# An attention block and a soft mixture of experts in one program: the attention's and the front's steps merged into one list an engine

## The reference, cut to what matters

```python
# attention (B=8, T=512, C=256, 16 heads, latent 32)
q_lat, k_lat, v_lat = (t @ w.T + b for each head)      # rope on q_lat and k_lat
q_for_k = q_lat @ wqk_w.T + wqk_b
att = softmax(mask(einsum('bhql,bhkl->bhqk', q_for_k, k_lat) * L ** -0.5))
y   = heads(einsum('bhqk,bhkl->bhql', att, v_lat) @ l2o_w.T + l2o_b)
x1  = layernorm(x + y @ cproj_w.T + cproj_b)
# soft mixture of experts
z      = layernorm(x1) ; xn = z * norm_g + norm_b
logits = einsum('bnd,esd->bnes', xn, layernorm(slot_embeds) * slot_g + slot_b)
dispatch = softmax(logits, over tokens) ; combine = softmax(logits, over all slots)
slots  = einsum('bnd,bnes->besd', xn, dispatch)
eout   = (gelu(slots @ Wg + bg) * (slots @ Wu + bu)) @ Wd + bd
out    = layernorm(x1 + einsum('bns,bso->bno', combine, eout))
```

## Time and profile before

| | before |
|---|---|
| time, median of 3 (us) | 1336.6 (1336.46 to 1337.25) |
| the profiled execution: time, span (us) | 1336.36, 1334.5 |
| TensorE matmul busy | 1215.3 us, 91% |
| VectorE, ScalarE, GpSimd busy | 61%, 51%, 34% |
| TensorE's mean granted clock | 0.96 |

### The profile page before, as it was taken

One profiled execution on the slowest core, in us unless ns is written; L12 is line 12 of the kernel. 1 busy time (PEld: TensorE's weight loads), 2 busy tenths in 40 slices (PEclk: granted clock), 3 DMA queues, 4 the chain that ended last, 5 costly groups with the idle time before them and its releaser, 6 DMA issues.

```text
span 1334.5 us, 19895 instructions
## 1 busy us (share of the span) xinstructions
PE 1215.3 (91%) x7190; PEld 944.3 (71%) x7222; DVE 814.2 (61%) x1318; ACT 682.2 (51%) x1042; POOL 449.5 (34%) x336
## 2 busy tenths in 40 slices
PE   5798999999999999973799999994999999999996
PEld 4465666666656666632688888883888888888885
DVE  3877697979787978631577777763444444432343
ACT  2545464646465656451667777762555555540111
POOL 5544555555545555410100000000444444430000
PEclk9898999999999999976899999997999999999998
DMA  3644353636363645411123333234554545453661
GB/s 121 139 104 111 90 158 87 163 90 159 89 157 91 158 97 134 107 49 63 48 95 111 111 112 112 96 104 152 195 165 166 164 166 165 165 193 95 225 247 47
DMA packets 121790, 170.30 MB, mean 128 GB/s; under 512 B 47025, under 2 KB 76146, under 8 KB 121714
## 3 DMA queue, kind: packets, MB, share of 16 engines
q1 hardware_dynamic: 120818, 168.74, 43.4%
q10 hardware_dynamic: 896, 0.56, 0.1%
HBM read 72.26 MB, written 37.75 MB: 82 GB/s over the span
## 4 chain that ended last, share of the span: by engine, by line
PE 51%; DVE 3%; ACT 2%; DMA 1%; issue 1%; POOL 1%; SPq 0%; ACTq 0%; POOLq 0%; DVEq 0%
PE ring L361 8%; PE ring L363 8%; PE ring L362 7%; PE ring L1438 6%; PE tail L361 3%; PE tail L363 3%; PE tail L362 3%; PE tail L1438 2%; PE ring L1365 2%; PE ring L1348 1%; PE ring L1355 1%; PE tail L1285 1%; PE ring L1274 1%; PE ring L1307 1%; PE tail L1355 1%
## 5 line engine op out<-in xcount | busy, mean ns | idle before, releaser
L738 ACT ACTIVATE pt<-ring 128x1024 f32<-128x1024 f32 (+1 forms) x192 | 169.2, 882 | 148.7 <-PE ring L1274 137.1
L983 DVE TENSOR_REDUCE mx<-ring 128x4 f32<-128x512 f32 (+2 forms) x192 | 197.7, 1039 | 77.6 <-PE ring L1259 77.3
L628 POOL TENSOR_SCALAR_AFFINE_SELECT pt<-pt 128x512 f32<-128x512 f32 x128 | 81.2, 634 | 248.2 <-ACT pt L738 248.2
L1274 PE MATMUL ring<-qks 98*128 98x256 f32 (+3 forms) x512 | 131.6, 361 | 10.3 <-DVE mx L983 4.8
L1257 PE MATMUL ring<-qks 96*128 96x384 f32 (+3 forms) x512 | 139.9, 362 | 0.9 <-DVE mx L983 0.6
L1274 PEld LDWEIGHTS ring<-qks 98*128 98x128 f32 x512 | 77.6, 195 | 69.1 <-DVE mx L983 28.8
L1285 PE MATMUL tail<-pt,va 128*32 128x512 f32 (+3 forms) x1024 | 99.8, 463 | 11.6 <-POOL pt L628 9.8
L653 POOL TENSOR_TENSOR hl<-hid,hh 128x512 fp32r<-128x512 f32 x64 | 82.6, 1302 | 78.4 <-ACT hh L824 78.4
L639 POOL TENSOR_TENSOR zl<-z,zh 128x1024 fp32r<-128x1024 f32 x8 | 19.3, 2410 | 242.9 <-ACT zh L777 242.9
L1257 PEld LDWEIGHTS ring<-qks 96*128 96x128 f32 x512 | 92.2, 199 | 10.9 <-ACT pt L738 6.1
L1097 DVE SCALAR_TENSOR_TENSOR hid<-ring,bias_e,gate 128x512 f32<-128x512 f32 x64 | 47.9, 748 | 83.3 <-ACT gate L818 51.9
(11 more groups left out here) (217 smaller groups left out, 3114.0 us busy)
## 6 DMA issues: line engine op xcount, KB each, us to landing
qks<-stg SPq DMA_DIRECT2D x384, 128.0 KB, 2.4
c_dram<-c2s SPq DMA_DIRECT2D x32, 512.0 KB, 5.2
c<-c_dram SPq DMA_DIRECT2D x32, 512.0 KB, 5.9
sl_dram<-sls SPq DMA_DIRECT2D x32, 256.0 KB, 3.4
sl<-sl_dram SPq DMA_DIRECT2D x16, 512.0 KB, 4.8
wg<-in_wg SPq DMA_DIRECT2D x16, 512.0 KB, 5.6
wu<-in_wu SPq DMA_DIRECT2D x16, 512.0 KB, 6.2
wd<-in_wd SPq DMA_DIRECT2D x16, 512.0 KB, 7.0
```

What stands on the lines that cost most here:

```text
L628: nc.gpsimd.affine_select(out=m, in_=m, compare_op=ALU.is_ge, fill=0.0, base=0, pattern=[[0, GH], [1, P]], channel_multiplier=-1).then_inc ...
L738: nc.scalar.activation(pt[j % 2][:, h:h + heads, 0:n], heads_of(tile, heads, n), ACT.Exp, scale=SCALE).then_inc(empty, 1)
L983: nc.vector.tensor_reduce(out=mx[:, g, i, h:h + heads], in_=heads_of(tile, heads, (i + 1) * P), axis=AX.X, op=ALU.max).then_inc(empty, 1)
L1274: last = nc.tensor.matmul(scores[:, h, :], qks[0:KS_ROWS + 2, g, h0 + h, 1, j * P:(j + 1) * P], qks[0:KS_ROWS + 2, g, h0 + h, 0, j * P:T], ...
```

## The change

`attn_order` becomes `order(at, window, start)`: it puts the steps of the front's windows at positions of their own, 16.3 a round, into the same sorted list. Each engine has a start for them (PE and SP 264, ACT 263, DVE 261), where attention of batch 7 has the positions from 224 on. The second loops over the front's steps go away on PE, ACT, DVE and SP; GpSimd keeps its own. Front steps thus stand among the steps of batch 7's groups: s1 of batch 0 among the exp of group 2, round 0 among those of group 3 and the projection, cproj, ln and apply of batch 7 in round 1.

`fills` numbers all fills together: the three ring places in turn, and the tail pair from the last misc or pv step on; the first fill of the tail waits until misc and ybank are drained. z is loaded once its own batch's store has landed, and the first two also once xt and v of batch 7 were read. SP's window has z behind the slots stores. New waits name the last readers of what lies under each front buffer, and the attention's and the front's buffers get new addresses, which set what those last readers are. The names quad_slot and quad_count become slot and fill_count throughout (not shown).

```diff
+FRONT_AT, FRONT_ACT_AT, FRONT_DVE_AT, FRONT_SPAN = 264, 263, 261, 16.3
...
-def attn_order(at):
+def order(at, window=(), start=FRONT_AT):
...
+    for w in range(-2, B + 1):
+        for n, (name, ahead, *more) in enumerate(window):
+            if 0 <= w + ahead < B:
+                todo.append((start + FRONT_SPAN * (w + n / len(window)), len(todo), (name, w + ahead, *more)))
     return [step for _, _, step in sorted(todo)]
 
 
-def front_order(window):
-
-    steps = []
-    for w in range(-1, B + 1):
-        for name, ahead, *n in window:
-            if 0 <= w + ahead < B:
-                steps.append((name, w + ahead, *n))
-    return steps
+def fills(steps):
+
+    free, left = list(range(RING)), [0] * QUAD
+    slot_of, turn_of = {}, {}
+    last = max(n for n, s in enumerate(steps) if s[0] in MISC_STEPS + ("pv",))
+    for n, s in enumerate(steps):
+        if n == last:
+            free.insert(0, RING)
+        if s[0] in PAIR_STEPS:
+            r = free.pop(0)
+            free.append(r)
+            slot_of[s], turn_of[s] = r, left[r]
+            left[r] += 1
+    return slot_of, turn_of, left
...
-SP_FRONT = (("z", 2), ("c2", 0, 0), ("c2", 0, 1), ("slots", -1, 1), ("slots", 0, 0), ("c2", 0, 2), ("c2", 0, 3))
-
-PAIR_STEPS = ("lat", "max", "exp", "v", "yTT", "cproj", "wv", "seT")
+SP_FRONT = (("c2", 0, 0), ("c2", 0, 1), ("slots", -1, 1), ("z", 2), ("slots", 0, 0), ("c2", 0, 2), ("c2", 0, 3))
+
+PAIR_STEPS = ("lat", "max", "exp", "v", "yTT", "cproj", "wv", "seT", "zT", "s1", "s2", "d", "c2", "slots")
...
+    pe_steps = order(PE_AT, PE_FRONT)
+    slot_of, turn_of, FILLS = fills(pe_steps)
+    misc_no = {s: n for n, s in enumerate(s for s in pe_steps if s[0] in MISC_STEPS)}
...
+    lat = place("lat", [P, 2, T], f32)
+    rot = place("rot", [P, 2, T], f32)
+    rope = place("rope", [P, 2, T], f32)
     cos = place("cos", [P, T], f32)
     sin = place("sin", [P, T], f32)
-    blat = place("blat", [P, 2, G], f32)
+    stg = [place(f"stg{i}", [P, 4, T], f32r) for i in range(2)]
+    qks = place("qks", [P, G, GH, 2, T], f32r)
+    mts = [place(f"mts{i}", [2 * GH, T], f32r) for i in range(2)]
+    identb = place("identb", [P, P], bf16)
+    maskb = place("maskb", [P, GH, P], bf16)
+    wq = place("wq", [P, P], f32)
     bwq = place("bwq", [P, 1], f32)
     bv = place("bv", [P, C], f32)
+    va = place("va", [P, NT, H, L], f32)
+    temp_at = at[0]
+    pt = [place(f"pt{i}", [P, GH, T], f32) for i in range(2)]
+    ys = place("ys", [P, T], f32)
+    ytok = place("ytok", [P, NT, C], f32)
+    yT_ = place("yT_", [P, NC, T], f32)
+    x = [place(f"x{i}", [P, NT, C], f32) for i in range(2)]
+    x1 = place("x1", [P, NT, C], f32)
...
+    s1s, c1, dh, dl = [], [], [], []
+
+    def rows_of(i):
+        s1s.append(place(f"s1s{i}", [P, NT, E * S], f32))
+        c1.append(place(f"c1{i}", [P, NT, E * S], f32))
+
+    def dispatch_of(i):
+        dh.append(place(f"dh{i}", [P, NT, 512], f32r))
+        dl.append(place(f"dl{i}", [P, NT, 512], f32r))
+
+    assert at[0] <= xt_at + 36 * KB
+    rows_of(0)
+    c2s = [place(f"c2s{i}", [P, 2, T], f32) for i in range(2)]
     e2 = [place(f"e2{i}", [P, 2, T], f32) for i in range(4)]
-    dh = [place(f"dh{i}", [P, NT, 512], f32r) for i in range(2)]
-    dl = [place(f"dl{i}", [P, NT, 512], f32r) for i in range(2)]
-    c2s = [place(f"c2s{i}", [P, 2, T], f32) for i in range(4)]
+    dispatch_of(0)
+    rows_of(1)
+    dispatch_of(1)
+    c2s += [place(f"c2s{i + 2}", [P, 2, T], f32) for i in range(2)]
     sls = [place(f"sls{i}", [P, NC, 512], f32) for i in range(2)]
-    m1 = place("m1", [P, 2, NT], f32)
-    cs = place("cs", [P, 2, NT], f32)
-    m2 = place("m2", [P, NT, 2], f32)
-    es = place("es", [P, NT, 2], f32)
-    res = place("res", [P, NT, 2], f32)
-    assert at[0] <= nc.sbuf_usable_end - 16 * KB
+    assert at[0] <= temp_at + 26 * KB
...
+    def last_read(engine, g):
+        read = ("exp", B - 1, g, len(EXP_UNITS) - 1)
+        engine.wait_ge(pair_filled[slot(read)], fill_count(read))
...
+            def load_z(b):
+                sp.wait_ge(z_stored, (b + 1) * 16)
+                sp.dma_start(z[b % 2][:, :, :], z_dram[b, :, :]).then_inc(z_loaded[b % 2], 16)
+
+            for st in order(SP_AT, SP_FRONT):
                 name, b = st[:2]
...
-            sp.wait_ge(z_stored, B * 16)
-            sp.wait_ge(x1_stored, B * 16)
-            load_z(0)
...
+                elif name == "z":
+                    if b < 2:
+                        for read in (("lat", B - 1, G - 1), ("v", B - 1)):
+                            sp.wait_ge(pair_filled[slot(read)], fill_count(read))
                         load_z(b)
                     else:
-                        sp.wait_ge(quad_filled[quad_slot(("zT", b - 2))], quad_count(("zT", b - 2)))
+                        sp.wait_ge(pair_filled[slot(("zT", b - 2))], fill_count(("zT", b - 2)))
                         sp.wait_ge(z_low, b - 1)
                         load_z(b)
...
-            for st in attn_order(ACT_AT):
+            for st in order(ACT_AT, ACT_FRONT, FRONT_ACT_AT):
...
+                    if (b, n) == (0, 0):
+                        act.wait_ge(cosed, B * G)
+                        act.wait_ge(roped, B * G)
+                        act.wait_ge(k_low, B * G)
+                        act.wait_ge(misc_filled, misc_count(("wqk", B - 1, G - 1)))
+                        for g in range(G):
+                            act.wait_ge(stacked[g], B * 3 * GH * 16)
+                    elif (b, n) == (1, 0):
+                        last_read(act, G - 1)
+                        act.wait_ge(y_filled, B * G)
                     nc.scalar.activation(s1s[b % 2][:, n, :].rearrange("p (k s) -> p k s", k=2), tile[:, :, :], ACT.Copy)
...
+                    if b == 0:
+                        last_read(act, n // 2)
...
+                    elif n < 2:
+                        last_read(act, 1)
+                    else:
+                        act.wait_ge(y_filled, B * G)
...
+                    if b == 0 and n < 2:
+                        last_read(act, 0)
+                    elif b == 0:
+                        act.wait_ge(y_filled, B * G)
+                        act.wait_ge(misc_filled, misc_count(("yT", B - 1, G - 1)))
...
-            for st in attn_order(DVE_AT):
+            for st in order(DVE_AT, DVE_FRONT, FRONT_DVE_AT):
...
+                    if b == 0 and n < 2:
+                        last_read(dve, 2)
+                    elif b == 0:
+                        dve.wait_ge(y_filled, B * G)
...
-            for st in attn_steps:
+            for st in pe_steps:
...
+                    if (slot(st), fill_count(st)) == (RING, 1):
+                        pe.wait_ge(misc_drained, len(misc_no))
+                        pe.wait_ge(y_drained, B * G)
...
-            for r in range(RING):
-                pe.wait_ge(pair_drained[r], FILLS[r])
-            pe.wait_ge(misc_drained, len(misc_no))
-            pe.wait_ge(y_drained, B * G)
-
-            for st in front_steps:
-                name, b = st[:2]
-                tile = quad[quad_slot(st)]
-                full = quad_filled[quad_slot(st)]
-                pe.wait_ge(quad_drained[quad_slot(st)], quad_count(st, 0))
-
-                if name == "zT":
+                elif name == "zT":
```

More of the change, by code:

```diff
@@ L173, in block_kernel @@
     snv, sny, snt, snm = (place(n, [P, 8], f32) for n in ("snv", "sny", "snt", "snm"))
-    temp_at = at[0]
-    pt = [place(f"pt{i}", [P, GH, T], f32) for i in range(2)]
-    ys = place("ys", [P, T], f32)
-    ytok = place("ytok", [P, NT, C], f32)
-    yT_ = place("yT_", [P, NC, T], f32)
-    x = [place(f"x{i}", [P, NT, C], f32) for i in range(2)]
-    x1 = place("x1", [P, NT, C], f32)
+    m1 = place("m1", [P, 2, NT], f32)
+    cs = place("cs", [P, 2, NT], f32)
+    m2 = place("m2", [P, NT, 2], f32)
+    es = place("es", [P, NT, 2], f32)
+    res = place("res", [P, NT, 2], f32)
     at[0] = temp_at
@@ L261, in block_kernel @@
     misc, ybank = tail[:, 0, :], tail[:, 1, :]
-    quad = ring + [tail]
+    pairs = ring + [tail]
     acc = ((ring[0], ring[1]), (ring[2], tail))
@@ L271, in block_kernel @@
     setup_dve = sem("setup_dve")
-    pair_filled = [sem(f"pair_filled{r}") for r in range(RING)]
-    pair_drained = [sem(f"pair_drained{r}") for r in range(RING)]
+    pair_filled = [sem(f"pair_filled{r}") for r in range(QUAD)]
+    pair_drained = [sem(f"pair_drained{r}") for r in range(QUAD)]
     misc_filled, misc_drained = sem("misc_filled"), sem("misc_drained")
@@ L288, in block_kernel @@
     z_loaded = [sem(f"z_loaded{i}") for i in range(2)]
-    quad_filled = [sem(f"quad_filled{r}") for r in range(QUAD)]
-    quad_drained = [sem(f"quad_drained{r}") for r in range(QUAD)]
     z_high, z_low, xn_high, xn_low = sem("z_high"), sem("z_low"), sem("xn_high"), sem("xn_low")
@@ L602, in _ @@
             pool.wait_ge(in_rope, IN_ROPE * 16)
-            for st in attn_order(POOL_AT):
+            for st in order(POOL_AT):
```

(9 more changed lines are left out.)

95 lines of the change are left out of this document (26 added, 69 removed).

## The result

The changed kernel takes 1329.59 us (median of 4 runs, 1328.13 to 1330.48) against 1336.92 us for the kernel before beside it (4 runs, 1336.46 to 1338.24): a ratio of 0.994, interval 0.9925 to 0.996. It is faster by 7.3 us, where 28.6 us were forecast and 1296 us was the low end of the range, 1322 the high end. The direction was right and the size was not. The profiled execution took 1329.52 us (span 1327.8), 6.8 us less than the one of before.

What follows compares the result with a forecast made beforehand. TensorE sets the pace except in a hole where latencies do. Work 99.95 us plus waits 26.9 us makes the 155.4 us stretch 126.8, a gain of 28.6, so 1308 us; range 1296 to 1322.

Steps and rivals of the forecast that it cites:

- I take full clock, since both gaps lie in dense work: TensorE's clock stays at 2.4 GHz through the merged stretch despite gaps at 565.8 and 579 us; nothing charged.
- The rival with the fallen clock: TensorE's clock falls in the merge, between 583 and 606 us: 9 us more, 1317 us; chance 0.18.
- zT(0) crossed on VectorE: VectorE has zT(0) ahead of max (7,2,5) and cproj(6), which TensorE fills in reverse order: 4.0 us of waits.
- layernorm of batch 6: On VectorE it comes some 4 us later, behind xn(0) as well, and holds exp (7,2,1): 3.0 us.
- s1 among the exp: Groups 2 and 3 with batch 0's s1 between the exp: ScalarE sets the pace, TensorE waits 3.9 us.
- z(1): SP issues its load behind batch 6's stores and x(7); lands near 606.5, wanted by zT(1) at 605.1: 1.0 us.
- round 0: Front's first round on three places, with group 3's exp and pv: waits of 7.6 us, plus 0.7 for zT(2).
- round 1: Takes in batch 7's tail (cproj, layernorm, apply) on VectorE and ScalarE, which holds up the front's steps: 5.9 us.
- e2: A step of the front's rounds; in round 1, batch 7's layernorm on VectorE delays its (1,1) by 2.0 us.
- Nothing: Items charged no time: new waits on last readers, GpSimd's x bias, masks and zl, new addresses, z(0)'s load.
- longer waits: In-order lists of three engines on three PSUM places: waits 1.4 times as long, 11 us more, 1319; chance 0.12.
- slower: z(b+2) behind the slots store makes every steady round wait, six rounds of 39 us: 1343 us; chance 0.03.

Runs made afterwards that it cites:

- experiment 8: Changed kernel with unused bf16 matmuls added in five of TensorE's waits: 1325.23 us, ratio 0.992.
- experiment 11: The kernel of experiment 7 with the apply and store of batch 6 later and x(7) loaded ahead of the stores: 1303.21 us, ratio 0.975.
- experiments 1 and 4: Changed kernel, GpSimd's x(7) bias and zl of batches 0 and 1 cut to one column: 1321.72 us; the same work moved, nothing left out: 1323.70 us.
- experiment 9: Changed kernel with only the layernorm of batch 6 moved later on VectorE, behind max(7,3,5): 1327.92 us, ratio 0.992.
- experiment 10: Changed kernel with only the layernorm of batch 7 moved later on VectorE, its apply and store behind it: 1323.61 us, ratio 0.989.
- after's second execution: Profiled execution of the changed kernel run once more, unaltered, as yardstick on another chip: median 1328.93 us, ratio 0.994.
- experiment 7: Changed kernel with zT(0) later on VectorE, z(1) earlier on SP, GpSimd's zl and bias spread, and both layernorms later: 1305.07 us, ratio 0.976.

## Why the prediction was right in direction and wrong in size

The forecast stretch was work 99.95 + waits 26.9 + nothing for the clock = 126.8 us. Measured are 104.0 + 31.0 + 11.7 = 146.7 us (idle time from the window; work at full clock and the half clock's part from 2 us windows, whose sum the window's busy time is). Of the 19.9 us missing, 11.7 are the clock, 4.1 the waits and 4.0 the work. The clock is the largest part and the wrong step; by itself it would have given 1320 us, inside the range, and it took one of the other two besides to leave it.

**The clock: the step that failed.** "I take full clock, since both gaps lie in dense work" is wrong. The reason given was one of the two rows against the other, and the changed kernel sided with the fall: behind the waits of 2.75 and 0.93 us, of 2.90, of 2.05 and 2.73, of 6.03 and of 4.19 us windows of 2 and 3 us have the clock at 0.50 to 0.54. Before had 13.6 us of half clock in this stretch, and the forecast counted them all as returned; after has 11.7. The rival with the fallen clock (0.18) was the right mechanism, put at 9 us and at 1317 us. Where it placed the fall, 583 to 606 us, it was low for some 3 us only; it was low also within 573 to 577, 610 to 618, 631 to 638, 641 to 645 and 689 to 696 us. That this costs time is shown by experiment 8 (waits filled, clock held behind them, 4.1 us) and by experiment 11 (no fall, 4.3 us less busy time for the same work). Two of the prediction's own signs of being wrong came: a clock of 0.50 between 570 and 606 us, and z(1) landing after 610. The rule of the Trainium skill that the prediction cited ("TensorE: Matmul & The Clock Gate", "A second HAM failure mode: psum-queue depth-cycling") spoke against the step taken, and the trace of after agrees with it: 0.50 behind a wait of 2.90 us. Not every such wait brings a fall: the clock stayed 1.00 through 2.69 us in the kernel before and 2.16 us in experiment 11. What decides stays open.

**The waits: right but for three.** By the prediction's terms, in us:

| term | forecast | measured on TensorE |
|---|---|---|
| zT(0) crossed on VectorE | 4.0 | 2.75 + 0.93 = 3.7 |
| layernorm of batch 6 | 3.0 | 2.90 |
| s1 among the exp | 3.9 | 2.05 + 0.45 + 0.21 = 2.7 |
| z(1) | 1.0 | 2.73 |
| round 0 | 8.3 | 12.5, of it 6.03 before d(0,0) |
| round 1 | 5.9 | 6.5, of it 4.19 before e2(1,1)'s transposes |

- *Round 0's 1.7 us "before d (0,0)" were 6.03*, and with them fell the sentence under *Nothing*, "POOL's x bias, masks and zl have long gaps ahead of them now". It asked whether GpSimd was late for its reader. It was not; but its line of three ran against VectorE's e2(0,0), as experiments 1 and 4 show (1.83 us without it). Round 0's other terms were 0.70 + 0.94 behind the c2 copies (forecast 0.9 + 1.1), 2.16 for s1 (1,0) (2.4), 0.85 at the new wait ahead of d (0,3) (0.8), 0.85 for zT(2) (0.7).
- *Round 1's 2.0 us for e2 (1,1) were 4.19*, since zl(2) holds one step of the layernorm for 2.3 us; slots (0,1) waited 0.40 instead of 1.6, cproj(7) 1.88 instead of 1.9.
- *z(1)* landed at 613.7 and was wanted at 611.0; the mechanism (behind the apply, then store, x, z through the same engines) was right. The apply ended at 605.8 us by its SP rows and not near 599.5, since all ahead of it was late.
- Layernorm 6's wait came as forecast, but taking it away by itself gained 0.4 us (experiment 9); taking away layernorm 7's gained 6.3 us, more than its wait (experiment 10).
- The rival *longer waits* had them 1.4 times as long; they were 31.0 / 26.9 = 1.15 times as long.

**The work: 99.95 forecast, 104.2 measured** by experiment 11 at clock 1.00. Its round 1 takes 35.38 us with waits of 1.9, 33.5 of work against 33.2 forecast, so nearly all of the 4 us lie ahead of zT(2), in what the walk put down for the rest of groups 2 and 3 and for round 0. The same count for the kernel before gives 115.0 − 13.6 = 101.4 us for the same groups: 1.4 us were too little already for the old order, and some 2.6 us came with the new one. Which lines were too small stays open.

**Right:** zT(0) near 565 us (567.55) without its 17 us wait; rounds of 33.2 us later on, z issued behind the stores with no wait on it in this stretch but z(1)'s (z(3) holds zT(3) for 0.22 us in after's second execution and 0.70 us in experiment 8); the new waits on last readers and the new addresses at nothing, but for 0.85 us ahead of d (0,3). Neither "slower" mechanism showed, nor did fewer waits. Wrong were PEclk 9 in all slices, zT(2) near 652 us (670.71) and zT(3) near 692 us (714.06).

The forecast's 28.6 us were in the change, though not as it was written: with ten steps on VectorE, ScalarE, SP and GpSimd put at other places, in the order in which TensorE fills and where VectorE is free of GpSimd, it gives 32 us (experiment 7).

## What to carry to other kernels

When two in-order lists are merged, walk not only who waits for whom, but for each moved step also who runs at the same time on VectorE and GpSimd: an SBUF-to-SBUF instruction on VectorE can last until GpSimd's instruction beside it ends (2.32 us instead of 0.17 here), one that reads PSUM did not. Price waits like those here (2 to 6 us) on TensorE at themselves plus some of the work behind them at half clock, since most of them brought a fall, though not all; put steps that drain PSUM in the order in which TensorE fills it, and bookkeeping such as a layernorm behind what TensorE waits for. Idle time that a reorder squeezes out need not return the clock: half clock took 13.6 us before, 11.7 after, 15.3 with ln(6) moved, 4.8 in experiment 7 and none in experiment 11. So test the fixes together as well as alone.

## What was unexpected of the hardware

- Two VectorE instructions over 512 columns took 5.09 us instead of 0.88, and one over 8 columns 2.32 us instead of 0.17, beside GpSimd instructions over 1024 columns of 2.35 to 2.5 us each. The ends fit turns of one: GpSimd's three end near 630.5, 633.0 (by halving the row of two) and 635.5 us, and VectorE's pair ends at 633.3 and xnl at 636.6, so that each VectorE instruction came behind one of GpSimd's.
- A wait of 2.90 us, and the pair of 2.75 and 0.93, were followed by 3 to 4 us at a clock of 0.50, that of 4.19 us by 6; and two profiled executions of the same kernel lost 11.7 and 14.0 us of the stretch to the half clock. Waits of 2.02 and 2.17 us in experiment 7 were followed by a clock of 0.50; of 1.22, 1.83 and 2.16 us in experiment 11 none was.
- Filling waits with matmuls that nobody reads was worth 4.1 us of 183 here; reordering, which removes many of the waits, was worth 23.
